# Layer norm statistics from row sums and one ScalarE square with a sum, in a fused cross-attention and linear-attention kernel

## What is computed

```python
# layer 0: softmax cross attention, 16 heads of 32
Q, K, V = x @ Wq.T + bq, ctx @ Wk.T + bk, ctx @ Wv.T + bv      # split into heads
att = softmax(Q K^T / sqrt(32)); out = (att @ V) @ Wo.T + bo
x = norm(out + x, gamma0, beta0)
# layer 1: linear attention with elu features
Qp, Kp = elu(x), elu(ctx); KV = Kp^T @ ctx
Z = 1 / (Qp . Kp.sum(axis=1) + 1e-6)
x = norm(x + (Qp @ KV) * Z, gamma1, beta1)
# norm(y): m = mean(y); v = mean((y - m)**2); (y - m) * rsqrt(v + 1e-5) * gamma + beta
```

## Time and profile before

| | |
|---|---|
| median of 3 runs (lowest to highest) | 1528.52 us (1524.69 to 1529.03) |
| the profiled execution | 1526.61 us |
| its span, first to last instruction | 1525.2 us |
| TensorE clock granted, mean | 0.988 |

### The profile page before, as it was taken

How to read it: one execution, slowest core, us unless ns; L and a number is a source line. 1 busy time by engine, 2 the same in 40 slices (tenths; PEclk the granted TensorE clock), 3 DMA queues, 4 the chain that set the end, 5 groups by cost and what they waited for, 6 DMA issues and landing times.

```text
span 1525.2 us, 30133 instructions
## 1 busy us (share of the span) xinstructions
PE 1481.1 (97%) x10528; PEld 1043.0 (68%) x10528; DVE 1297.9 (85%) x2509; ACT 826.7 (54%) x1595; POOL 1237.8 (81%) x1100
## 2 busy tenths in 40 slices
PE   8999999999999999999999999999999999999886
PEld 6767767676767777667676767666767667756554
DVE  6687888778898988987898897989789889988886
ACT  2454655555555555665555555655555555555542
POOL 0486787767899898967888898877889898897995
PEclk9999999999999999999999999999999999999998
DMA  7744254433325244243344326235242434410001
GB/s 223 212 134 135 70 161 128 148 110 111 111 85 149 79 130 148 77 127 120 96 126 128 104 85 179 91 101 141 87 130 86 145 112 116 130 51 27 7 22 42
DMA packets 159574, 170.14 MB, mean 112 GB/s; under 512 B 20288, under 2 KB 122048, under 8 KB 159424
## 3 DMA queue, kind: packets, MB, share of 16 engines
q1 hardware_dynamic: 157696, 167.16, 36.7%
q10 hardware_dynamic: 1728, 1.05, 0.2%
HBM read 125.97 MB, written 42.21 MB: 110 GB/s over the span
## 4 chain that ended last, share of the span: by engine, by line
PE 83%; DVE 5%; POOL 5%; issue 3%; DMA 2%; ACT 1%; SPq 1%; POOLq 0%; DVEq 0%; ACTq 0%
PE score L465 15%; PE scoreT L479 14%; PE acc L497 13%; PE misc L540 7%; PE misc L552 7%; PE misc L516 7%; PE misc L529 7%; PE misc L577 6%; PE misc L569 4%; POOL pair_sum L1044 2%; PE acc L506 2%; DVE maxes L778 1%; DVE pair_sum L818 1%; POOL pair_sum L1053 1%; PE misc L560 1%
## 5 line engine op out<-in xcount | busy, mean ns | idle before, releaser
L643 ACT ACTIVATE p_ring<-scoreT 128x512 f32<-128x512 f32 x1024 | 597.6, 595 | 552.2 <-PE scoreT L479 546.3
L1044 POOL TENSOR_TENSOR pair_sum<-p_ring 128x512 f32<-128x512 f32 x512 | 665.5, 1308 | 173.1 <-ACT p_ring L643 106.9
L778 DVE TENSOR_REDUCE maxes<-score 128x1 f32<-128x512 f32 x1024 | 678.8, 678 | 114.9 <-PE score L465 108.7
L465 PE MATMUL score<-k_stack,q_stack 96*128 96x512 f32 x1024 | 601.9, 589 | 6.8 <-DVE maxes L778 5.1
L479 PEld LDWEIGHTS scoreT<-q_stack,k_stack 104*128 104x128 f32 x2048 | 390.0, 192 | 155.9 <-ACT p_ring L643 80.1
L479 PE MATMUL scoreT<-q_stack,k_stack 104*128 104x256 f32 x2048 | 421.9, 288 | 7.1 <-ACT p_ring L643 6.6
L465 PEld LDWEIGHTS score<-k_stack,q_stack 96*128 96x128 f32 x1024 | 193.5, 189 | 164.4 <-issue 101.5
L1053 POOL TENSOR_TENSOR pair_sum<-pair_sum 128x512 f32<-128x512 f32 x192 | 253.3, 1319 | 0.0
L497 PE MATMUL acc<-p_ring,v_sb 128*32 128x256 f32 x4096 | 250.1, 385 | 0.0
L818 DVE TENSOR_TENSOR pair_sum<-pair_sum 128x512 f32<-128x512 f32 x192 | 216.7, 1129 | 5.8 <-POOL pair_sum L1044 5.8
L497 PEld LDWEIGHTS acc<-p_ring,v_sb 128*32 128x32 f32 x4096 | 120.8, 110 | 85.4 <-issue 3.5
(11 more groups left out here) (95 smaller groups left out, 1361.8 us busy)
## 6 DMA issues: line engine op xcount, KB each, us to landing
xT_sb<-xT_in SPq DMA_DIRECT2D x63, 512.0 KB, 3.9
q_stack<-q_dram SPq DMA_DIRECT2D x189, 128.0 KB, 2.5
k_stack<-k_dram SPq DMA_DIRECT2D x93, 256.0 KB, 4.4
ctx_nat<-ctx_in SPq DMA_DIRECT2D x32, 256.0 KB, 4.2
q_dram<-q_high SPq DMA_DIRECT2D x63, 128.0 KB, 1.7
q_dram<-q_low SPq DMA_DIRECT2D x63, 128.0 KB, 1.9
k_dram<-k_high SPq DMA_DIRECT2D x31, 256.0 KB, 2.0
k_dram<-k_low SPq DMA_DIRECT2D x31, 256.0 KB, 2.2
```

The source lines that it names most:

```text
L465: pe.matmul(score[k % 3][:], q_stack[0:SPLIT, unit % NQ, j, t * P:(t + 1) * P], k_stack[0:SPLIT, group_of[unit] % 2 * QUAD + j, h * HALF:( ...
L643: act.activation(p_ring[:, n % NP, h * HALF:(h + 1) * HALF], scoreT[k % 2][:], ACT.Exp, scale=SCALE).then_inc(A["exped"], 1)
L778: dve.reduce_max(maxes[:, unit % 2, t, j, h:h + 1], score[k % 3][:], AX.X).then_inc(V["maxed"], 1)
L1044: pool.tensor_tensor(pair_sum[:, place_of_pair(pair), cols], p_ring[:, (n - 1) % NP, cols], p_ring[:, n % NP, cols], ALU.add).then_inc(L[" ...
```

## The change

The statistics of a norm no longer come from `bn_stats` and `bn_aggr`. The instruction that makes the tile now also gives the sum of each row: for `sum_y` the plain addition becomes a `scalar_tensor_tensor` (times 1.0, plus x) with `accum_out`, and `attend` gets `accum_out` too. Directly behind it, in the same tick, DVE multiplies the sum by `-ROOT / D` (ROOT is 1/sqrt(512)), which gives the negative mean times ROOT. ACT then squares the tile with scale ROOT and that bias, and sums over the row: that sum is the variance. Its elementwise output goes into `x_nat`, where nobody needs it. POOL's `root` adds epsilon itself, waits for that, and goes on as before. `centre`, on the five norms that end on DVE, first turns the mean back to its own scale and now waits for ACT's square. The planner books one ACT step of cost 8 in place of two DVE steps of 7 and 4, and counts 10 and 11 in place of 7 and 8 for DVE in the last tick of `O` and `A`.

```diff
         def finish_norm(tile, norm, k):
-            k = book(f"count{norm}", "DVE", k + 1, 7, tile)
-            k = book(f"aggregate{norm}", "DVE", k + 1, 4, tile)
+            k = book(f"square{norm}", "ACT", k + 1, 8, tile)
             rooted = book(f"root{norm}", "POOL", k + 1, 8, tile)
...
-            cost = {... "O": (0, 7), "T": (6, 8), "A": (0, 8), ...
+            cost = {... "O": (0, 10), "T": (6, 8), "A": (0, 11), ...
...
+            def square(tile, norm):                                  # ACT
+                s = slot_of[tile]
+                act.wait_ge(V[f"mean_made{norm}"], tile + 1)
+                act.activation(x_nat[s], y_sb[s], ACT.Square, scale=ROOT, bias=neg_mean[:, s, :],
+                               accum_out=var[:, s, :]).then_inc(A[f"squared{norm}"], 1)
...
-                dve.tensor_tensor(y_sb[slot_of[tile]], bank_of("O", tile)[:], x_nat[slot_of[tile]],
-                                  ALU.add).then_inc(V["y_summed"], 1)
+                dve.scalar_tensor_tensor(out=y_sb[slot], in0=bank_of("O", tile)[:], scalar=1.0, in1=x_nat[slot],
+                                         op0=ALU.mult, op1=ALU.add,
+                                         accum_out=sums[:, slot, :]).then_inc(V["y_summed"], 1)
+                dve.wait_ge(V["y_summed"], tile + 1)
+                make_mean(tile, 0)
+
+            def make_mean(tile, norm):
+                s = slot_of[tile]
+                dve.tensor_scalar(neg_mean[:, s, :], sums[:, s, :], -ROOT / D, None,
+                                  ALU.mult).then_inc(V[f"mean_made{norm}"], 1)
...
-            def count(tile, norm):       # bn_stats
-            def aggregate(tile, norm):   # bn_aggr, then var_eps = variance + epsilon
...
             def centre(tile, norm):
                 s = slot_of[tile]
-                dve.wait_ge(V[f"var_added{norm}"], tile + 1)
+                dve.wait_ge(V[f"mean_made{norm}"], tile + 1)
+                dve.tensor_scalar(centre_at[:, s, :], neg_mean[:, s, :], 1.0 / ROOT, None,
+                                  ALU.mult).then_inc(V[f"mean_back{norm}"], 1)
+                dve.wait_ge(V[f"mean_back{norm}"], count_of(tile, norm))
+                dve.wait_ge(A[f"squared{norm}"], tile + 1)
...
             def root(tile, norm):                                    # POOL
                 s = slot_of[tile]
-                pool.wait_ge(V[f"var_added{norm}"], tile + 1)
+                pool.wait_ge(A[f"squared{norm}"], tile + 1)
+                pool.tensor_scalar(var_eps[:, s, :], var[:, s, :], LN_EPS, None,
+                                   ALU.add).then_inc(L[f"var_added{norm}"], 1)
+                pool.wait_ge(L[f"var_added{norm}"], tile + 1)
                 pool.tensor_tensor(rstd[:, s, :], var_eps[:, s, :], minus_half[:],
                                    ALU.pow).then_inc(L[f"rooted{norm}"], 1)
```

More of the change, by code:

```diff
@@ L25, in build @@
     LN_EPS, ATTN_EPS = 1e-5, 1e-6
+    ROOT = float(D) ** -0.5
     SPLIT = 3 * DK
@@ L124, in build @@
         max_turned = sb("max_turned", [P, 2, DK])
-        stats = sb("stats", [P, NX + 4, 6])
-        mean_var = sb("mean_var", [P, NX + 4, 2])
+        sums = sb("sums", [P, NX + 4, 1])
+        neg_mean = sb("neg_mean", [P, NX + 4, 1])
+        centre_at = sb("centre_at", [P, NX + 4, 1])
+        var = sb("var", [P, NX + 4, 1])
         var_eps = sb("var_eps", [P, NX + 4, 1])
@@ L153, in build @@
         A = sems("warmed", "k_high_kept", "q_high_kept", "exped", "v_kept", "kv_high_kept", "ksum_kept", "f_below", "f_grown", "normal0",
-                 "below", "grown", "phiT_high_kept", "normal1", "first_from_act")
+                 "below", "grown", "phiT_high_kept", "normal1", "squared0", "squared1", "first_from_act")
         V = sems("hot_rows", "phiT_low_kept", "kv_low_kept", "k_low_kept", "q_low_kept", "maxed", "max_whole", "max_high", "max_low", "max_split", "max_turned", "pad_cleared",
                  "run_high", "den_turned", "den_inverted", "den_back", "out_scaled", "f_phi", "y_summed",
-                 "counted0", "aggregated0", "var_added0", "phi_made", "dotted", "z_added", "z_inverted",
-                 "y_attended", "counted1", "aggregated1", "var_added1", "bias_spread", "bias_folded",
+                 "mean_made0", "mean_back0", "phi_made", "dotted", "z_added", "z_inverted",
+                 "y_attended", "mean_made1", "mean_back1", "bias_spread", "bias_folded",
                  "centred0", "centred1", "x1_on_dve", "result_on_dve", "first_from_dve")
-        L = sems("cleared", "hot", "ident_made", "ones_made", "half_made", "paired", "run_low", "totalled", "biased", "rooted0",
+        L = sems("cleared", "hot", "ident_made", "ones_made", "half_made", "paired", "run_low", "totalled", "biased", "rooted0", "var_added0", "var_added1",
                  "shifted0", "scaled0", "x1", "rooted1", "shifted1", "scaled1", "result")
@@ L323, in follow @@
             end = end_of[kind, i]
-            cost = {"K": (6, 8), "V": (6, 0), "Q": (5, 5), "O": (0, 7), "T": (6, 8), "A": (0, 8), "S": (6, 8),
+            cost = {"K": (6, 8), "V": (6, 0), "Q": (5, 5), "O": (0, 10), "T": (6, 8), "A": (0, 11), "S": (6, 8),
                     "N": (6, 0), "B": (0, 7)}[kind]
@@ L760, in scalar_program @@
                 for norm in range(2):
+                    if k in when[f"square{norm}"]:
+                        square(when[f"square{norm}"][k], norm)
                     if k in when[f"normalise{norm}"]:
@@ L878, in sum_y @@
                     dve.wait_ge(T["bias_passed"], 1)
-                dve.tensor_tensor(y_sb[slot_of[tile]], bank_of("O", tile)[:], x_nat[slot_of[tile]],
-                                  ALU.add).then_inc(V["y_summed"], 1)
-            def count(tile, norm):
-                s = slot_of[tile]
[L884 to L888, removed]
@@ L890, in aggregate @@
-            def aggregate(tile, norm):
[L891 to L896, removed]
+                slot = slot_of[tile]
@@ L898, in centre @@
             def centre(tile, norm):
                 s = slot_of[tile]
-                dve.wait_ge(V[f"var_added{norm}"], tile + 1)
-                dve.scalar_tensor_tensor(out=y_sb[s], in0=y_sb[s], scalar=mean_var[:, s, 0:1],
-                                         in1=(gamma0_row, gamma1_row)[norm][:], op0=ALU.subtract,
+                dve.wait_ge(V[f"mean_made{norm}"], tile + 1)
+                dve.tensor_scalar(centre_at[:, s, :], neg_mean[:, s, :], 1.0 / ROOT, None,
+                                  ALU.mult).then_inc(V[f"mean_back{norm}"], 1)
@@ L903, in centre @@
+                dve.wait_ge(V[f"mean_back{norm}"], count_of(tile, norm))
+                dve.wait_ge(A[f"squared{norm}"], tile + 1)
+                dve.scalar_tensor_tensor(out=y_sb[s], in0=y_sb[s], scalar=centre_at[:, s, :],
+                                         in1=(gamma0_row, gamma1_row)[norm][:], op0=ALU.add,
                                          op1=ALU.mult).then_inc(V[f"centred{norm}"], 1)
@@ L937, in attend @@
                 dve.scalar_tensor_tensor(out=y, in0=bank_of("A", tile)[:], scalar=z_sb[:, tile % 2, 2:3], in1=y,
-                                         op0=ALU.mult, op1=ALU.add).then_inc(V["y_attended"], 1)
+                                         op0=ALU.mult, op1=ALU.add,
+                                         accum_out=sums[:, slot_of[tile], :]).then_inc(V["y_attended"], 1)
+                dve.wait_ge(V["y_attended"], tile + 1)
+                make_mean(tile, 1)
             def keep_phiT_low(tile):
@@ L1007, in vector_program @@
                 for norm in range(2):
[L1008 to L1012, removed]
                     if k in when[f"centre{norm}"]:
@@ L1069, in root @@
                 pool.wait_ge(L[f"rooted{norm}"], tile + 1)
-                pool.tensor_scalar(shift[:, s, :], mean_var[:, s, 0:1], rstd[:, s, :], -1.0, ALU.mult,
+                pool.tensor_scalar(shift[:, s, :], neg_mean[:, s, :], rstd[:, s, :], 1.0 / ROOT, ALU.mult,
                                    ALU.mult).then_inc(L[f"shifted{norm}"], 1)
```

## The result

The changed kernel takes 1521.03 us (median of 16 runs, 1517.2 to 1527.37) against 1527.42 us for the kernel before (16 runs). The ratio is 0.9964, with a 95% interval of 0.9953 to 0.9974: 5.5 us less. (The two medians alone differ by 6.4 us; the text goes by the ratio throughout.) The forecast's sum was 2.0 us less, its time 1525.5 us. The measured time lies in the range. At 0.36% it is a little beyond the bound of 0.3% on the faster side, though the interval reaches to both sides of that bound, so the outcome is, narrowly, the one that was given 0.32. It came for a reason that the forecast had put at nothing.

The account below looks back on a forecast made before the run. PE sets the pace nearly everywhere. -6 (DVE) + 0 (ACT) + 3.7 (POOL) + 0.3 (end) = -2.0 us on 1526.6 gives 1524.6, by the median 1526.5; forecast 1525.5, between the two, range 1514 to 1537.

Parts of the forecast that it names:

- the one that was given 0.32: Whole kernel: the outcome of being faster than before by more than 0.3%, 4.6 us; chance 0.32.
- DVE, -6 us: DVE's norm statistics: 47 us less busy time would take 6 us off the kernel, between 4.2 and 11.6.
- Half of the upper end: DVE term: 6 us, half of 11.6 us, as ACT is next late after about half the gain.
- My walk through DVE's busy stretches: PE's waits for maxima, shrunk by DVE work removed ahead in each busy stretch: 11.6 of 52.2 us would go.
- ACT, 0 us: ACT's square, sum read and wait for the mean, between exponentials: hidden behind two ticks, costing 0.
- rival 3: ACT's square overruns its cover, delaying exponentials in empty ticks; decides from 0.76 us with its sum; 1539 us; chance 0.10.
- POOL, +3.7 us: POOL's epsilon step in root: ten roots on the chain at 0.37 us each, ends 2.7 and 8.3.
- The last norms, +0.3 us: Norms behind the last attention unit: centre waiting for ACT and the very last norm ending later add 0.3 us.
- The plan, 0 with 3 us either way: Planner's ticks: phi jumps eight ticks or stays, last-batch A and T hold each other; worth 0, 3 us either way.
- Rival 1: DVE's relief reaches PE in full, 11.6 us, POOL's additions hide, some T chains come earlier: 1515 us; chance 0.20.
- Rival 6: Nothing changes where it counts: DVE's relief and POOL's addition turn into waiting, 1526.6 to 1528.5 us; chance 0.11.
- Rivals 4 and 5: Sums halve the two DVE instructions' rate, 1532 us, chance 0.06; square and exponential reload ACT tables, 1612 us, chance 0.03.

Follow-up runs that it names:

- experiment 1: The change's new operations on the tick plan of the kernel before, the square in the tick of count: ratio 1.0012 to the kernel before.
- The lighter count: The kernel before with bn_stats over 64 of the 512 columns, everything else as before: ratio 0.9995.
- experiment 5: The kernel before with ACT's square and its sum added, result unused, waiting for the tile alone and not for the mean: ratio 1.0000.
- experiment 3: The kernel before with one more tiny tensor_scalar, adding zero to the variance, and a wait for it in every POOL root: ratio 1.0070, 10.7 us.
- experiments 10 and 11: Kernel before with aggregate in the tick of count: 0.9994; new operations on the old plan with the square in the tick of aggregate: 1.0023.
- experiment 2: The old operations on the changed kernel's plan, both DVE statistics steps in the tick booked for the square: ratio 0.9990 to the kernel before.
- experiment 10: The kernel before, operations and plan, with aggregate in the tick of count instead of one to five ticks later: ratio 0.9994.

## Why the prediction was right, point by point

In short: the number was right and the account was not. The sum of -2.0 us was a sum of operations, with the plan at 0; these operations on the old plan measured +1.8 us (experiment 1). The plan turned the sign.

**DVE, -6 us: the step was mis-sized.** The busy time came out nearly as said (1251 forecast, 1258 in the profile; read, mean and `attend` within 5 ns, `sum_y` 689 ns where 741 was forecast), but not what it is worth. The lighter count won 0.05% for 21 us; the new operations without the POOL step 0.18%, 2.7 us. "Half of the upper end", 6 us, lies outside the interval of that run (0.9 to 4.6 us); the chain's own 4.2 us lies in it. My walk through DVE's busy stretches let a wait of PE shrink and the next one stay. PE's waits did fall as forecast, to 45.4 us, but time taken off such a wait is not time taken off the kernel: the maxima, freed of the statistics, wait for PE instead, 130.7 us in the changed kernel against 108.7.

```profile
L788 DVE TENSOR_REDUCE maxes<-score 128x1 f32<-128x512 f32 x1024 | 675.0, 678 | 136.2 <-PE score L467 130.7
```

**ACT, 0 us: right for the square**, by experiment 5; the wait for the mean was not run apart. The read of the sum was taken from DVE's row and was 0.19 us instead of 0.08, so square and read together are 0.91 us, past the 0.76 us at which I let rival 3 decide; it didn't decide there. That bound treated every norm as if empty ticks followed it, back to back. The comparison of ends gave 15 waits for the mean, up to 0.66 us and 5.8 us in all, while attention runs. The changed kernel has fewer and longer ones between 100 and 1440 us, 5.0 us in all:

```profile
ACT tiles L684 <- DVE neg_mean L898: 5.0, 8, 2.0
```

**POOL, +3.7 us: in size right for the changed kernel** (4.7 and 4.6 us), and three times too small for the kernel before (10.7 us), from whose trace it was worked out. Counted from exponential 256 on, the kernel of experiment 3 is 10 to 11 us longer in the table, half of it behind the last exponential (50.8 to 56.2); without the step the end goes from 50.2 to 45.5 and from 50.1 to 45.9 us. The mean step was 0.386 us; the power behind it became shorter, 0.604 against 0.695 us. Counting the roots on the chain did not give the price, since the step itself brings more roots onto the chain (6 to 12 of the 14 late ones).

**The last norms, +0.3 us: neither shown nor refuted.** The end of the changed kernel is bound as the forecast's last items said, with epsilon on the chain three times:

```profile
1506.76 0.77 ACT tiles L684 x2
...
1507.60 0.56 POOL var_eps L1070
...
1513.15 0.20 POOL var_eps L1070
...
1517.89 0.64 POOL var_eps L1070
...
1519.28 0.75 DVE ctxT_sb L916
```

**The plan, 0 with 3 us either way: this step failed.** It is worth 7.3 us with the new operations (0.48%, give or take 0.15), more than the whole difference. The rule I argued from is true: while maxima run, `phi` finds room only in visits and jumps eight ticks or stays. But 14 of 32 jumped. I had followed the last batch, where `A` and `T` do hold each other in place (from `T` 24 on, all of them end in the same ticks in both plans, and the last-batch booking alone gives 1.0009), and took it for the whole. The booking of the first 24 tiles fixes where all chains go.

So the forecast of -2 us was right in its range and its sign by luck, by errors that partly cancelled: DVE 3 us too good and POOL 1 us too cheap on one side, the plan 7 us too poor on the other.

Three of the signs named beforehand spoke against the account. "If the waits of PE for DVE fall without the span falling" came true in experiment 1 (52.2 to 46.9 us, at 1.0012). "If the plan moves the last batch's chains" came true for six of them: the four `S` chains of batch 3 end 7 to 21 ticks earlier, `O` 24 and 25 two ticks later. And ACT's square, which was to be on the chain only in the last 40 us, is there at 427 and 883 us too. PE's weight load waits for exponentials for 87.3 us in place of 80.1, below rival 3's mark of 10 us more; in experiment 5 it was 82.8 at no cost.

Of the rivals, none held as a whole. Rival 1 had the right event, "a few `T` chains come a visit earlier", beside a price that came from DVE's relief. Rival 6, 1526.6 to 1528.5 us, is what the operations do alone (1.0012 times 1526.6 is 1528.4), but POOL's addition did not go into waiting. Rivals 4 and 5 fell at once: both sums run at 0.69 and 0.75 us, and the trace has one table load of 1.283 us with squares in it. Neither rule of the Trainium skill came into play. The one of the Trainium skill, "Vector Engine (DVE) Microarchitecture Reference", "Points that are easy to get wrong", speaks of two sources in SBUF; with one in PSUM the trace shows no halving. By the Trainium skill, "ScalarE: Activation LUTs", "Table sets: the hidden batching unit", functions of different sets need a load at each switch; a single load in a kernel with squares and exponentials means that there was no such switch here.

**What stays open.** Why the POOL step costs 10.7 us with the old operations and 4.6 us with the new ones: not the late variance (experiments 10 and 11). That DVE's statistics and POOL's step lengthen one alternating path, and so cost more together than apart, fits the trace of experiment 3, but no kernel tried it by itself. Nor is it known why the plan is worth less with the old operations (0.10%) than with the new (0.48%). Each ratio has an interval of 0.1% to each side, so the difference of 0.38% has about 0.2% and is clear of the noise; yet from exponential 256 on the profile of experiment 2 is as much shorter than that of before (3.6 us) as the changed kernel's than experiment 1's (3.9 us). Experiment 2 also puts both statistics steps into one tick, which experiment 10 shows to be harmless on the old plan only.

## What to carry to other kernels

Where a planner places the work, a change of one operation is a change of the plan: run the new operations on the old plan and the old ones on the new plan before crediting either. Relief on an engine that waits elsewhere for the bound one was worth about a tenth of its busy time or less here (0.8 us for 21, 2.7 for 37). A new tiny step on the engine that carries the end of the kernel cost 10.7 us in one kernel and 4.6 in another, against 3.7 by the count on the chain, though that engine was idle for 19% of the span; the count on the chain is no fixed number. So ask which engine has idle time at the end before placing a step as small as adding epsilon: on ACT in place of POOL it measured 0.17% less, with intervals that overlap.

## What the runs showed of the hardware

The read of a sum is not the same on both engines: 82 ns on DVE, 191 ns on ACT. A sum over the row costs DVE's scalar_tensor_tensor with one operand in PSUM nothing beyond that read (746 ns with it, 741 without), and the same instruction with a factor of 1.0 takes no longer than a plain addition (689 and 691 ns). ACT took 42 us of squares and sums without any effect on the time (1.0000).

A tiny instruction on POOL has two durations. Of the 64 epsilon steps of the changed kernel 41 took 0.21 to 0.32 us and 23 took 0.55 to 0.77, about 0.44 us more. 20 of the 23 began while DVE ran an instruction of over 0.4 us that reads SBUF alone, against 5 of the 41. Here is one of each kind, the first beside a DVE sum of pairs, the second with DVE idle (start us, us, engine):

```profile
1454.76 1.75 DVE L828 TENSOR_TENSOR pair_sum<-pair_sum 128x512 f32<-128x512 f32 x1 [0.57 <-POOL pair_sum L1049]
...
1455.93 0.66 POOL L1070 TENSOR_SCALAR var_eps<-var 128x1 f32<-128x1 f32 x1
...
1513.12 0.22 POOL L1070 TENSOR_SCALAR var_eps<-var 128x1 f32<-128x1 f32 x1
```

It is a coincidence in time, and no run tried it by itself. The two durations account for the shorter power too. Alone in `root`, in the kernel before, the power took 0.54 to 0.59 us 43 times and 0.93 to 1.07 us 21 times; behind the epsilon step it took 0.56 to 0.57 us 58 times and over 0.85 only 6 times. The undisturbed power is no shorter (medians 548 and 567 ns); the first of the two instructions takes the disturbance. With the gap of 0.07 to 0.10 us between them, the step's net price on POOL is about 0.3 us.
